# A transformer decoder on one core: weighted values of two head groups per TensorE burst, one ring of exponentials, and a place of their own for the last weights

## The reference, cut to what matters

```python
x = ln(x + L0_attn(x))          # 16 heads of 8, rotary, softmax
x = ln(x + L0_xattn(x, ctx))    # 16 heads of 8, cross attention
x = ln(x + L0_ffn(x))           # mixture of 8 experts, top 2, all experts computed
x = ln(x + L1_attn(x))          # one causal head of width 128
x = ln(x + L1_xattn(x, ctx))    # 16 heads of 8, cross attention
x = ln(x + L1_ffn(x))           # 8 experts, top 1, capacity 128 tokens each
# in each of the three 16-head attentions, for head h:
score = einsum('bhqd,bhkd->bhqk', Q, K) / sqrt(8)
out   = einsum('bhqk,bhkd->bhqd', softmax(score), V)
```

## Time and profile before

| | us |
|---|---|
| median of 3 executions | 458.1 |
| lowest and highest | 455.65 and 461.03 |
| the profiled execution, its own time | 458.44 |
| its span, first to last instruction | 456.6 |

### The profile page before, as it was taken

How to read it: one execution, slowest core, us unless ns; L and a number is a source line. 1 busy time by engine, 2 the same in 40 slices (tenths; PEclk the granted TensorE clock), 3 DMA queues, 4 the chain that set the end, 5 groups by cost and what they waited for, 6 DMA issues and landing times.

```text
span 456.6 us, 9057 instructions
## 1 busy us (share of the span) xinstructions
PE 393.9 (86%) x3284; PEld 337.0 (74%) x3284; DVE 280.7 (61%) x829; ACT 242.2 (53%) x551; POOL 48.1 (11%) x57
## 2 busy tenths in 40 slices
PE   1589999899999999999979999999999698874292
PEld 1577778687778998889968989878898576643292
DVE  2477887978874547732676554685543983934444
ACT  2226567676676654676447566576573265451141
POOL 6200000940000000000000000000001020020115
PEclk9969999999999999999979999999999899996597
DMA  7605311031512000002001002000002002650300
GB/s 270 186 23 143 91 24 42 6 90 31 165 45 47 1 2 1 1 3 46 2 6 41 2 1 47 2 1 1 1 2 59 0 12 71 186 172 0 102 13 31
DMA packets 18907, 22.53 MB, mean 49 GB/s; under 512 B 2984, under 2 KB 13361, under 8 KB 18864
## 3 DMA queue, kind: packets, MB, share of 16 engines
q1 hardware_dynamic: 17344, 18.68, 15.1%
q10 hardware_dynamic: 1008, 2.31, 1.5%
q0 software_dynamic: 512, 0.97, 0.7%
HBM read 13.63 MB, written 2.11 MB: 34 GB/s over the span
## 4 chain that ended last, share of the span: by engine, by line
PE 74%; DVE 14%; issue 5%; ACT 3%; DMA 1%; POOL 0%; POOLq 0%; SPq 0%; DVEq 0%; ACTq 0%
PE bank_D L812 13%; PE bank_C L703 10%; PE bank_D L677 9%; PE bank_A L688 9%; DVE negmax L1190 4%; PE bank_A L828 4%; PE bank_A L830 3%; PE bank_A L829 3%; PE bank_A L619 3%; PE bank_K L599 3%; PE bank_A L620 2%; PE bank_A L1484 2%; PE bank_D L663 2%; PE bank_D L732 1%; PE bank_A L742 1%
## 5 line engine op out<-in xcount | busy, mean ns | idle before, releaser
L1190 DVE TENSOR_REDUCE negmax<-bank_D 128x2 f32<-128x512 f32 x192 | 127.2, 685 | 33.9 <-PE bank_D L677 33.6
L964 ACT ACTIVATE expo<-bank_A 128x512 f32<-128x512 f32 x192 | 110.8, 597 | 46.5 <-PE bank_A L688 44.6
L677 PE MATMUL bank_D<-k_head,q_sp 128*128 128x256 f32 x384 | 93.3, 331 | 5.0 <-DVE negmax L1190 2.5
L1000 ACT ACTIVATE hidden<-bank_A,b 128x256 f32<-128x256 f32 x128 | 53.7, 471 | 59.4 <-PE bank_A L830 59.3
L688 PE MATMUL bank_A<-q_sp,k_head 128*128 128x256 f32 x384 | 81.4, 297 | 1.9 <-DVE q_sp L1185 1.5
L677 PEld LDWEIGHTS bank_D<-k_head,q_sp 128*128 128x128 f32 x384 | 61.8, 199 | 20.2 <-issue 9.5
L812 PE MATMUL bank_D<-mix_w,hidden 128*128 128x128 f32 x512 | 69.4, 278 | 1.1 <-DVE ctx_n L1117 1.1
L812 PEld LDWEIGHTS bank_D<-mix_w,hidden 128*128 128x128 f32 x512 | 62.3, 191 | 7.2 <-issue 5.8
L688 PEld LDWEIGHTS bank_A<-q_sp,k_head 128*128 128x128 f32 x384 | 60.0, 193 | 5.4 <-DVE q_sp L1185 2.9
L703 PE MATMUL bank_C<-expo,v_aug 128*32 128x256 f32 x768 | 51.4, 385 | 1.9 <-ACT expo L964 1.7
L1249 DVE SCALAR_TENSOR_TENSOR y_mixture<-bank_D,g_w,y_mixture 128x128 f32<-128x128 f32 x64 | 22.4, 350 | 45.7 <-PE bank_D L812 45.6
(11 more groups left out here) (180 smaller groups left out, 534.2 us busy)
## 6 DMA issues: line engine op xcount, KB each, us to landing
k_head<-k_sp SPq DMA_DIRECT2D x96, 64.0 KB, 2.0
mix_w<-in_mix_w SPq DMA_DIRECT2D x24, 256.0 KB, 3.2
expo<-in_mix_w SPq DMA_DIRECT2D x6, 256.0 KB, 3.6
proj_w<-in_proj ACTq DMA_DIRECT2D x1, 640.0 KB, 11.4
xe_scratch<-empty_row SPq DMA_DIRECT2D x1, 520.0 KB, 5.2
expo<-xe_scratch SPq DMA_DIRECT2D x2, 260.0 KB, 3.4
expo<-in_spread SPq DMA_DIRECT2D x1, 512.0 KB, 7.9
expo<-in_spread ACTq DMA_DIRECT2D x1, 512.0 KB, 8.5
```

The lines of the kernel that those rows point to most:

```text
L677: last = mm(where(seq, b, ("max", k))[:, qt * SEQ:(qt + 1) * SEQ], q_sps[SET[seq, b]][:, k // 4, qt * P:(qt + 1) * P], k_heads[SET[seq, b] ...
L964: activate(expos[SET[seq, b]][:, h % ESLOTS, :], where(seq, b, ("exp", h))[:], ACT.Exp, scale=float(HD) ** -0.5).then_inc(free(seq, b, ("e ...
L1000: last = activate(hidden[:, (e % 2) * FC + f, :], where(seq, b, ("up", n))[:, i * SEQ:(i + 1) * SEQ], ACT.Relu, bias=b1[:, e * FC + f:e * ...
L1190: V.tensor_reduce(negmaxes[SET[seq, b]][:, s // 4, :, 32 * (s % 4)], where(seq, b, ("max", s))[:].rearrange("p (q n) -> p q n", q=QT), AX. ...
```

## The change

Two neighbouring groups are multiplied in one burst of 32 records, eight sets of four, at steps 17 and 25 instead of 13, 17, 21 and 25. It waits for the exponential of head 8p + 7, again issued two steps earlier. One ring `expo` of 12 slots serves all blocks in order, in place of two of 6; `pair_done` counts bursts over all blocks and takes the place of the four `group_done`. ACT's copies to `ctx_sb` stay at steps 17 and 25. The name `w1_last` is laid over the memory of `w1_lo` (whose allocation is given back at once), the last mixture's w1 is loaded there, and SP's wait before it is for the last `up` of the last first-layer mixture. SP's work at the first weighted values of block 3 moves from its step 13 to its step 17.

```diff
@@ -45,7 +45,7 @@
 CAP = TOKENS // EXPERTS
 SETS = 2
 EPS = 1e-5
-ESLOTS = 6
+ESLOTS = 12
 MASKED = -3.0e38
 
 
@@ -71,7 +71,7 @@
 OWN_VALUES_AT = -4
 SHIFT_AT = 6
 EXP_AT = 8
-VALUES_AT = 13
+VALUES_AT = 17
 BACK_AT, CTX_AT, OUT_AT, ROOT_AT, NORM_AT, TURN_AT = 26, 28, 30, 31, 32, 34
 ATTENTION_STEPS = range(KEYS_AT, TURN_AT + 1)
 
@@ -94,6 +94,7 @@
 MIXTURE = [(0, MIX0, 83), (1, MIX0, 103), (2, MIX0, 131), (3, MIX0, 156)]
 SET = {(seq, b): i % SETS for i, (seq, b, _) in enumerate(ATTENTION)}
 BEFORE = {(seq, b): ATTENTION[i - SETS][:2] for i, (seq, b, _) in enumerate(ATTENTION) if i >= SETS}
+ORDER = {(seq, b): i for i, (seq, b, _) in enumerate(ATTENTION)}
 NEXT_TO = {(seq, b): ATTENTION[i - 1][:2] for i, (seq, b, _) in enumerate(ATTENTION) if i >= 1}
 
 
@@ -124,6 +125,12 @@
 
     t, rest = divmod(step - start, 4)
     return t if rest == 0 and 0 <= t < GROUPS else None
+
+
+def pair_at(step, start):
+
+    pair, rest = divmod(step - start, 8)
+    return pair if rest == 0 and 0 <= pair < GROUPS // 2 else None
 
 
 def head(t, g):
@@ -174,8 +181,8 @@
                 turn(seq, b, ("max", s), "D")
             if 0 <= s - EXP_AT < HEADS:
                 turn(seq, b, ("exp", s - EXP_AT), "A")
-            if group_at(s, VALUES_AT) in (0, 2):
-                turn(seq, b, ("pv", group_at(s, VALUES_AT) // 2), "C")
+            if pair_at(s, VALUES_AT) is not None:
+                turn(seq, b, ("pv", pair_at(s, VALUES_AT)), "C")
             yield
 
     def mixture(seq, b):
@@ -276,7 +283,9 @@
         b2 = sb("b2", [EXPERTS, P])
 
         w1_hi = sb("w1_hi", [P, EXPERTS, HID], f32r)
-        w1_lo = sb("w1_lo", [P, EXPERTS, HID], f32r)
+        with nc.sbuf_tensor("w1_lo", [P, EXPERTS, HID], f32r) as w1_lo:
+            pass
+        w1_last = sb("w1_last", [P, EXPERTS, HID])
         mix_w2 = sb("mix_w2", [P, EXPERTS, FC, P])
 
         x_rows = sb("x_rows", [P, TILES, ROW])
@@ -314,7 +323,7 @@
         q_sps = sets("q_sp", [P, GROUPS, SEQ], f32r)
         v_augs = sets("v_aug", [P, QT, HEADS, 32])
         negmaxes = sets("negmax", [P, GROUPS, QT, P])
-        expos = sets("expo", [P, ESLOTS, QT * SEQ])
+        expo = sb("expo", [P, ESLOTS, QT * SEQ])
         ctx_sbs = sets("ctx_sb", [P, 2, SEQ])
 
         k_sp = sb("k_sp", [P, GROUPS, SEQ], f32r)
@@ -375,7 +384,7 @@
         k_head_ready = [[sem(f"k_head_ready{i}_{half}") for half in range(2)] for i in range(BATCH)]
         split_q_ready = [sem(f"split_q_ready{i}") for i in range(BATCH)]
         high_ready = [sem(f"high_ready{i}") for i in range(BATCH)]
-        group_done = [sem(f"group_done{i}") for i in range(BATCH)]
+        pair_done = sem("pair_done")
         x_hi_ready = sem("x_hi_ready")
         split_k_ready = [sem(f"split_k_ready{i}") for i in range(BATCH)]
         var_ready = [sem(f"var_ready{i}") for i in range(BATCH)]
@@ -428,8 +437,11 @@
             eng.wait_ge(free(seq, block, what), TURNS[seq, block, what][2] + 1)
 
 
-        staging = expos[0][:, 0:4, :].rearrange("p a (t c) -> p a t c", t=GROUPS)
-
+        staging = expo[:, 0:4, :].rearrange("p a (t c) -> p a t c", t=GROUPS)
+
+
+        def exp_slot(seq, block, h):
+            return (HEADS * ORDER[seq, block] + h) % ESLOTS
 
         def v_column(v_aug, odd, lo, hi):
 
@@ -475,12 +487,10 @@
                 nc.vector.memset(before[:, 0, :], 0.0)
 
 
-        last_w1 = [expos[0][:, e, :] for e in range(ESLOTS)] + [
-            negmaxes[0][:].rearrange("p t q n -> p (t q n)")[:, i * HID:(i + 1) * HID]
-            for i in range(EXPERTS - ESLOTS)]
+        last_w1 = [w1_last[:, e, :] for e in range(EXPERTS)]
         last_mixture = last_mixture_programs(nc, stack, out, dict(
             const=const, x_rows=x_rows, xe_dram=xe_dram, w1=last_w1, w2=mix_w2, banks=bank,
-            drained=drained, xe=expos[1], xeT=xT_all, x_norm=cT_all, ye=v_augs[1], ye_norm=v_augs[0],
+            drained=drained, xe=expo, xeT=xT_all, x_norm=cT_all, ye=v_augs[1], ye_norm=v_augs[0],
             hid=hidden, ident=ident, scattered=scattered, w1_loaded=w1_loaded, w2_loaded=w2_loaded))
 
 
@@ -568,7 +578,7 @@
                         sp.wait_ge(w1_split, what[1] // 2 + 1)
                         load(mix_w2[:, what[1] // 2], "mix0_w2", what[1] // 2, w2_loaded)
                     elif (seq, b) == ATTENTION[3][:2] and what == ("pv", 0):
-                        sp.wait_ge(group_done[seq], GROUPS * MHA[b] + 1)
+                        sp.wait_ge(pair_done, 2 * ORDER[seq, b] + 1)
                         sp.dma_start(b1[:], ins["b1"]).then_inc(ld_mix_biases, 16)
                         sp.dma_start(b2[:], ins["b2"]).then_inc(ld_mix_biases, 16)
                         sp.wait_ge(empty_row_ready, 1)
@@ -582,8 +592,7 @@
                         load(mix_w2[:, what[1] // 2], "mix1_w2", what[1] // 2, w2_loaded)
                     elif (seq, b) == ATTENTION[-1][:2] and what[0] == "exp" and what[1] % 2 == 0:
                         if what[1] == 0:
-                            last, block_before = ATTENTION[-2][:2]
-                            sp.wait_ge(group_done[last], GROUPS * (MHA[block_before] + 1))
+                            wait_filled(sp, *MIXTURE[-1][:2], ("up", 2 * EXPERTS - 1))
                         e = what[1] // 2
                         load(last_w1[e], "mix1_w1", e, w1_loaded)
                 last_mixture["sync"](sp)
@@ -690,22 +699,23 @@
                                   q_sps[SET[seq, b]][:, t, :], start=True, stop=True)
                     last.then_inc(full(seq, b, ("exp", h)), 1)
 
-                def weighted_values(seq, b, t):
-
-                    pair, odd = t // 2, t % 2
-                    if t == 0:
+                def weighted_values(seq, b, pair):
+
+                    if pair == 0:
                         wait_drained(pe, seq, b, "v")
-                    if odd == 0:
-                        wait_free(pe, seq, b, ("pv", pair))
-                    wait_drained(pe, seq, b, ("exp", 4 * t + 3))
-                    for kt in range(QT):
-                        for g in range(4):
-                            last = mm(where(seq, b, ("pv", pair))[32 * g:32 * g + 32, 0:SEQ],
-                                      v_augs[SET[seq, b]][:, kt, head(t, g), :],
-                                      expos[SET[seq, b]][:, (4 * t + g) % ESLOTS,
-                                                         kt * SEQ:(kt + 1) * SEQ],
-                                      start=(odd == 0 and kt == 0), stop=(odd == 1 and kt == QT - 1))
-                    last.then_inc(group_done[seq], 1)
+                    wait_free(pe, seq, b, ("pv", pair))
+                    wait_drained(pe, seq, b, ("exp", 8 * pair + 7))
+                    for odd in range(2):
+                        t = 2 * pair + odd
+                        for kt in range(QT):
+                            for g in range(4):
+                                last = mm(where(seq, b, ("pv", pair))[32 * g:32 * g + 32, 0:SEQ],
+                                          v_augs[SET[seq, b]][:, kt, head(t, g), :],
+                                          expo[:, exp_slot(seq, b, 4 * t + g),
+                                               kt * SEQ:(kt + 1) * SEQ],
+                                          start=(odd == 0 and kt == 0),
+                                          stop=(odd == 1 and kt == QT - 1))
+                    last.then_inc(pair_done, 1)
 
                 def back(seq, b):
                     wait_drained(pe, seq, b, ("pv", 1))
@@ -770,8 +780,8 @@
                             score_by_query(seq, b, s)
                         if 0 <= s - EXP_AT < HEADS:
                             score_by_key(seq, b, s - EXP_AT)
-                        if group_at(s, VALUES_AT) is not None:
-                            weighted_values(seq, b, group_at(s, VALUES_AT))
+                        if pair_at(s, VALUES_AT) is not None:
+                            weighted_values(seq, b, pair_at(s, VALUES_AT))
                         yield
 
                 def mixture(seq, b):
@@ -958,18 +968,18 @@
                         if 0 <= s - EXP_AT < HEADS:
                             h = s - EXP_AT
                             wait_filled(act, seq, b, ("exp", h))
-                            if h >= ESLOTS:
-                                act.wait_ge(group_done[seq],
-                                            GROUPS * MHA[b] + (h - ESLOTS) // 4 + 1)
-                            activate(expos[SET[seq, b]][:, h % ESLOTS, :],
+                            if HEADS * ORDER[seq, b] + h >= ESLOTS:
+                                act.wait_ge(pair_done,
+                                            (HEADS * ORDER[seq, b] + h - ESLOTS) // 8 + 1)
+                            activate(expo[:, exp_slot(seq, b, h), :],
                                      where(seq, b, ("exp", h))[:], ACT.Exp, scale=float(HD) ** -0.5
                                      ).then_inc(free(seq, b, ("exp", h)), 1)
```

(14 more changed lines are left out.)

## The result

| | us | against before, with 95% interval |
|---|---|---|
| forecast | 452.5 (449.0 to 457.5) | |
| changed kernel, 12 runs | 456.96 median, 453.33 to 457.98 | 0.9941 (0.9916 to 0.9966) |
| kernel before, beside it, 12 runs | 459.66 median, 455.65 to 462.55 | |
| changed kernel again, another chip, 6 runs (g1) | 455.52 median | 0.9904 (0.9867 to 0.9941), before 459.60 |
| profiled execution of the changed kernel | 456.41, span 454.6 | |

The kernel became faster, by 2.7 us in the first measurement and 4.1 in the second, where 5.9 had been forecast. The time alone lies inside the range; the gain is 0.6% and 1.0%, against a forecast of 1.3%. So the question is where two to three microseconds went.

What follows compares the result with a forecast made beforehand. TensorE was taken as the bound, 74% of the chain, but only where others wait for it. The terms -3.2 - 2.7 + 0.9 - 0.85 gave -5.9 us, from about 458.4 to 452.5 us, range 449.0 to 457.5.

Steps and rivals of the forecast that it cites:

- blocks 5 to 9: Ten pairs beside the mixture, taken as TensorE-bound: 0.32 us each, 3.2 us won, low end 2.5.
- block 11: End of the chain, where longer bursts delay the last exponentials' work: 0.9 us lost, between 0.5 and 1.5.
- The price of a switch: Each burst's cost of going from whole array to column tiles and back on TensorE: 0.32 us, saved once per pair.
- Blocks 0 to 4: Ten attention pairs, five winning 0.32 us and five 0.22 us each: 2.7 us won, from 1.6 to 3.9.
- Rival A: DVE and ACT set the pace in blocks 0 to 4, 10 and 11 and keep the gain: 455.7 us, chance 0.22.
- Blocks 0 to 9 together: The two terms for blocks 0 to 4 (2.7 us) and 5 to 9 (3.2 us), both won.
- Block 10: Some waits of DVE and ACT behind the removed bursts go: 0.85 us won, between -1.5 and +0.5.
- Rival C: The granted clock moves: half-speed stretches lost (448 us) or added on dense work (454.2, two 456), chance 0.13 either way.
- Rival B: Long bursts starve DVE at 14 merged bursts of blocks 0 to 4, 10 and 11: slower, 461.5 us, chance 0.08.
- The bounds: The range given for the whole kernel's time by the bounds of the parts: 448.6 to 456.4 us.

Runs made afterwards that it cites:

- e2: Changed kernel with merged bursts in blocks 0 to 9 only, four bursts in blocks 10 and 11: 454.92 us, 0.9908 of the kernel before.
- e3: Changed kernel with merged bursts in blocks 10 and 11 only, four bursts in blocks 0 to 9: 459.65 us, 1.0034 of the kernel before.
- f4: Changed kernel with no pair merged and each burst halved by key tile, adding 36 switches: 466.69 us, 1.0183 of the kernel before.
- f3: Changed kernel with blocks 10 and 11 and the second pair of block 8 left unmerged: 452.33 us, 0.9857 of the kernel before.
- g3: Changed kernel plus a redundant burst of group 0 at step 13 of block 11: 454.06 us, 0.9879 of the kernel before.
- f1: Changed kernel with only the first pair of block 11 left as two bursts: 453.55 us, 0.9915 of the kernel before.
- e1: Changed kernel (ring of 12, one counter) with no pair merged, four bursts a block: 457.74 us, 0.9997 of the kernel before.
- e4: Changed kernel with only the second pair of block 11 left as two bursts: 456.38 us, 0.9957 of the kernel before.
- g4: f1 run once more, only the first pair of block 11 left unmerged in the changed kernel: 453.57 us, 0.9880 of the kernel before.
- f2: Changed kernel with merged bursts in blocks 0 to 10 and four bursts in block 11: 452.92 us, 0.9875 of the kernel before.
- g2: Changed kernel with block 11 and the second pair of block 8 left unmerged: 451.41 us, 0.9823 of the kernel before.

## Why the prediction was wrong, step by step

Two steps of the sum failed: blocks 5 to 9 and block 11. By the times, merging in blocks 0 to 9 brought 4.2 us where 5.9 were forecast (e2; 2.6 to 5.8), and merging in the last two lost 1.6 where the forecast had 0.05 (e3; 0.1 to 3.0). The two gaps of 1.7 and 1.5 make up the missing 3.2 us.

- **The price of a switch, 0.32 us: right.** A merged burst takes what was worked out to 0.01 us, and f4 found 0.34 by adding switches.
- **Blocks 0 to 4, 2.7 us: too low.** The lead grew by 0.41 us a pair in all traces with merging there (3.3 us in eight pairs, to within 0.03 in the ten traces with all of these merged). Only at the second pair of block 4, which runs into the first mixture, did the lead that stood at step 4 shrink, by 0.3. The banks of pool D did cover the long burst, and waits for DVE that used to stand between bursts went under it.
- **Rival A, and the rule beside it: out for these blocks.** The long stretches have DVE at 93 and 99% and still hand the gain on. The "PSUM Bottleneck" section of the Trainium skill's "TensorEngine Tiling (Array Packing)" says that emptying PSUM may become the bottleneck; read as rival A reads it, nothing would have come here, and these rows disagree. Of the stretches shown, DVE became the limit in one only, at 8.38 of 8.49 us, after the gain had been taken.
- **Blocks 5 to 9, 3.2 us: the first step that failed.** 1.7 us arrived, and it was outside the low end of 2.5. "TensorE-bound: 10 x 0.32" was said of a whole stretch from one row at 158 us. It holds for seven of ten pairs. At the second pair of block 8 the removed burst stood beside a wait, and merging cost 0.85 us there, which f3 bears out; at the first pairs of blocks 6 and 7 it brought 0.14 and about -0.2, and why was not looked into. I had priced such places in block 11 and had not looked for them here.
- **Blocks 0 to 9 together, 5.9 us: too high.** The lead of 5.3 us at step 4 of block 10 looks like it, but 0.6 of it stood already at step 4 of block 1. From there the lead grew by 4.7 us, in the other traces with these blocks merged by 4.4 to 4.8, and e2's times say 4.2. The 0.6 us or so that blocks 0 to 4 brought over their term do not make up for what blocks 5 to 9 lack.
- **Block 10, -0.85: near in size, but from other parts.** Merging is worth 1.1 us there against splitting. The sum had 0.75 for the burst of step 13 and 0.1 for that of step 21; the traces show some 0.3 up to the burst of step 17 and 0.84 between it and the one of step 25. The profile of before had lost little to its stretch at 363 us, so the two profiles side by side showed a loss of 0.46.
- **Block 11, +0.9: the second step that failed.** "The burst that goes from step 13 brings nearly nothing, since DVE's routing work is waited for behind it" was right as a sum of instructions (1.32 us from L688 to L887 with the burst, 1.26 from L697 to L897 without), and wrong in what follows. With the wait that it leaves on TensorE the clock goes down just ahead of the scores that ACT waits for: 1.08 us by g3 against g1, about 1 over all profiles. The instruction part, 0.9, is 1.09 in g3: 0.94 for the first pair and 0.14 for the second, as in f1.
- **Rival C, the clock, had been treated as luck.** It said "either way", as if stretches at half speed moved at random, and it counted two of them where the profile of before has six (they begin at 21.6, 31.8, 233.2, 362.9, 414.1 and 451.6 us). Some do move: stretches near 21 to 35 and 227 to 240 us come and go from profile to profile, in merged and split kernels alike. One near 83 us stands in e1 and e3 alone, where blocks 0 to 9 are split, but not in the kernel before. The one at 395 us does not: it is in all four traces with the first pair of block 11 merged and no burst at step 13 (the changed kernel, g1, e3, e4), and in none of the other ten.
- **Rival B, starvation of DVE: out as a rule.** Of the ten pairs that it named in blocks 0 to 4, only the one at the end of block 4 lost time beside DVE, 0.3 us; block 10 gains by merging, and block 11 loses by other causes.
- **The bounds.** The parts as written add up to 450.3 to 456.3 us and not to 448.6 at the low end. The measured 456.96 lies above both sums.

What stays open: in the changed kernel 6 of 12 runs, in e4 5 of 12, in f1 4 of 11 and in g4 2 of 6 form a group at 457.2 to 458.0 us with a mean clock of 0.939 to 0.943, most at 0.939. None of e2, f2, f3, g2 and g3 has a run below 0.945, but neither has g1, which is the changed kernel itself. e1 has one run of 12 at 0.943 and e3 three; the kernel before has 5 of 32, 1 of 16 and 3 of 11 below 0.945 on the three chips of the experiments, down to 0.935. So a low mean clock is not peculiar to merging. No run of this group was profiled. e4 has only the place at 395 us and f1 only the one before the last burst, and both have such runs. A drop of 0.015 of the mean clock over 455 us is, by estimate, some 14 us more at half speed, so it must be more than one stretch of 3.4 us; which ones was not seen. g1 and g3 have no such run in six each, too few to say. Why the clock falls at one wait and not at another like it is not shown either: the 1.06 us before the last burst passed at full clock in f1 and in the changed kernel, and not in g4.

## What to carry to other kernels

Work that is taken out of a program in engine order is worth its time only where the engine is the bound at that very instruction, so follow a removed burst to the next wait behind it, place by place, and leave it where it stood beside a wait: merging 21 of 24 pairs beat merging all by 4 us. Before the last exponentials of a chain, mind the long pieces: one there can run wholly at the lower clock, as one profile (g4) shows. And when two profiles are compared, take the lead at many points along the program and use more than one profile of each kernel, since a stretch at half speed in one of them is as large as the effect.
